# Graph attention, GRU and expert layer: hT's low half first at a tile's end on VectorE, and the normalised x remade on ScalarE

## The chip, the cores and the metric

The kernel runs on one core of a Trainium2 chip. The metric is the device time of one execution in microseconds (us), shown as the median of several executions. The engines are TensorE (PE; PEld are its weight loads), VectorE (DVE), ScalarE (ACT), GpSimd (POOL) and SyncE (SP, which here only issues DMAs). Each runs its own instructions in the order in which they are written, and waits for the others through counted semaphores.

## What is computed

x is 4096 x 256, adj a 4096 x 4096 matrix of zeros and ones. The part that the change touches, with F = 256:

```python
h = layernorm(x)
Wh = h @ W
e = leaky_relu(Wh @ a[:F] + (Wh @ a[F:]).T, 0.2)
att = softmax(where(adj > 0, e, -9e15), axis=1)
h_prime = att @ Wh
gi = h_prime @ w_ih.T + b_ih
gh = h @ w_hh.T + b_hh
r = sigmoid(i_r + h_r); z = sigmoid(i_z + h_z); n = tanh(i_n + r * h_n)
x = x + (1 - z) * n + z * h
# then: layernorm, gate, the top 2 of 16 experts for each token,
# silu(x @ w1) * (x @ w2) @ w3 for each, weighted and added to x
```

## The kernel before

**Tiles and stages.** A first stage normalises x, forms the values and the two terms of the attention logits. The main stage goes over T = 32 tiles of 128 rows, i = 0 to 31, and ends at about 790 us of the span. After it come the routing and the expert products; the change does not touch them.

**Lag.** The main stage is a software pipeline. In iteration i the engines work on the attention of tile i, the logits and the masks of tile i+1, the GRU input of tile i-1 (`combine`, `remake_xn`, `transpose_h`, `copy_hT`, `hT_lo`), the GRU products and the output x1 of tile i-2 (`gru`, `gru_logits`, `gru_n`, `gru_out`), its second layernorm (`norm2`), and the gate of tile i-3 (`transpose_x2`, `copy_x2T`, `gate`, `route_top`, `route_weights`).

**Chunks.** Each tile's attention weights go in CPT = 8 chunks of 512 columns. PE transposes a chunk (L1092), ACT copies its high half to pc (`chunk_hi`, L488), DVE makes its low half (`chunk_lo`, L767, pc<-bank,pc), and PE multiplies it by the values in three terms (L1192 to L1194). Transposes, `chunk_hi` and `chunk_lo` run two chunks ahead of the products: at step c of iteration i, DVE makes chunk c+2, so that steps 6 and 7 make chunks 0 and 1 of the next tile.

**GRU.** PE starts an iteration with `gru(i)`: 12 products of 128x512 (L1218) and 12 of 128x256 (L1223). They read hT, which has a high half (ACT, `copy_hT`) and a low half (DVE, `hT_lo`, L793), made in step 6 of the iteration ahead. hT comes from a transpose of h_prime (hp) and xnb, the normalised x of the tile. xnb is remade from x, which SP loads again from memory (L351), since the first stage's copy was scaled.

**Second layernorm.** `norm2` takes statistics of x1 (L828, L829), writes the variance (var, L830), waits for POOL's power -0.5 (rs, L440), and writes the normalised row xrow (L834). PE transposes it after `gru` (`transpose_x2`).

**Order.** It is written out by hand: the body functions of each engine list what is issued in each step. The last tile and the three iterations behind it are written out separately. Instructions of one engine that depend on each other wait for the writer through `link`.

Of the kernel before, what the change touches and what calls it, by code (L numbers as in the profile page):

```python
# [29 lines left out]
P = 128  # L30
# [5 lines left out]
def gnn_moe(nc, x, adj, W, a, w_ih, w_hh, b_ih, b_hh, gate_w, gate_b, w1, w2, w3, out, rows):  # L36
# [24 lines left out]
    with ctx:  # L61
# [51 lines left out]
        rstd = sb("rstd", [P, T], F32, gs)  # L113
        sS = sb("sS", [P, T], F32, gs)
        bD = sb("bD", [P, T], F32, gs)
        bst = sb("bst", [P, 4, 6], F32, gs)
# [103 lines left out]
        s_plo = sem("weights_lo_done")  # L220
        s_mm = sem("chunk_accumulated")
        s_hp = sem("h_prime_done")
        s_xb = sem("xn_remade")
# [263 lines left out]
        def _(act):  # L487
# [88 lines left out]
            def n_tanh(i):  # L576
                act.wait_ge(s_np, i - 1)
                nc.scalar.activation(nn[:, 0:F], nn[:, 0:F], ACT.Tanh).then_inc(s_nt, 1)

            def copy_hT(i):  # L580
                act.wait_ge(s_th, i)
                if i >= 2:
                    act.wait_ge(s_gru, i - 1)
                act_copy(hT[:, 0, :, :].rearrange("p k m -> p (k m)"), tp[:, :]).then_inc(s_hT, 1)
# [9 lines left out]
            def body(i):  # L594
                if i + 1 < T:
                    for q in range(Q):
                        logits(i + 1, q)
                if live(i, 3):
                    copy_x2T(i)
# [19 lines left out]

            last = (T - 1) * CPT  # L620
            copy_x2T(T - 1)
            chunk_hi(last + 2)
# [11 lines left out]
            gate_exp(T)  # L634
            n_tanh(T)
            copy_hT(T)
            copy_x2T(T + 1)
# [59 lines left out]
        def _(dve):  # L697
# [97 lines left out]

            def remake_xn(n):
                v = n % 2
                dve.wait_ge(s_xr[v], (n // 2) * 16 + 16)
                V_.tensor_scalar(xnb[:, v, :], xin[:, v, :], xmv[:, n, 0:1], rstd[:, n:n + 1], ALU.subtract,
                                 ALU.mult).then_inc(s_xb, 1)  # L800

            def gru_logits(i):
# [21 lines left out]

            def norm2(i):
                u = i % 2
                dve.wait_ge(s_x1, i - 1)
                link(V_.bn_stats(bst[:, 0, :], x1))  # L828
                link(V_.bn_aggr(mv[:, :], bst[:, 0, :]))  # L829
                V_.tensor_scalar(var[:, :], mv[:, 1:2], EPS, None, ALU.add).then_inc(s_var2, 1)  # L830
                dve.wait_ge(s_rs2, i - 1)
                if i >= 4:
# [46 lines left out]
            dve.wait_ge(s_bld, 64)  # L879
            link(V_.tensor_tensor(bias_rz[:, :], bias_rz[:, :], bhh_rz, ALU.add))  # L880
            chunk_lo(0)
            chunk_lo(1)

            def body(i):
# [4 lines left out]
                if live(i, 1):  # L889
                    combine(i - 1)  # L890
                    remake_xn(i - 1)
                if ahead:
# [5 lines left out]
                for c in range(CPT):  # L898
# [13 lines left out]
                    if c == 5 and live(i, 2):  # L912
                        gru_out(i)
                    if c == 6 and live(i, 2):
                        norm2(i)
                    if c == 6 and live(i, 1):
                        hT_lo(i)
                    if i == 0:
                        for n in range(max(2 * c, 5), min(2 * c + 2, 13)):
                            weights_lo(n)  # L920
# [5 lines left out]
            combine(T - 2)  # L926
            remake_xn(T - 2)
            chunk_lo(last + 2)
# [8 lines left out]
            hT_lo(T - 1)  # L937
            chunk_lo(last + 6)
            norm2(T - 1)
            chunk_lo(last + 7)  # L940
            gru_logits(T)
            route_top(T)
            gru_n(T)
            combine(T - 1)
            remake_xn(T - 1)
            route_weights(T)
            hT_lo(T)
            gru_out(T)
            norm2(T)
            gru_logits(T + 1)  # L950
            route_top(T + 1)
            gru_n(T + 1)
            route_weights(T + 1)
            gru_out(T + 1)
            norm2(T + 1)
            route_top(T + 2)
# [434 lines left out]
```

## Time and profile before

| what | value |
|---|---|
| median of 3 runs | 1272.8 us |
| the three runs | 1272.82, 1268.34, 1272.80 us |
| the profiled execution, its own time | 1271.41 us |
| its span | 1269.7 us |
| PE busy in the span | 1158.3 us, 91% |
| DVE busy | 1044.5 us, 82% |
| ACT busy | 777.3 us, 61% |
| POOL busy | 354.0 us, 28% |

The span is what the trace covers, 1.7 us less than the execution's own time. Busy time is the sum of an engine's instructions; shares are of the span. Times in rows are in us from the span's start. A row of the timeline has start, duration, engine, line, operation, output<-input with shapes, a count where several are merged, and in brackets how long the engine sat idle before it and what ended that. Durations of neighbours on one engine can overlap a little, so the distance between two starts tells what an instruction takes of its engine. TensorE's granted clock is 1.00 of its full rate in the main stage's steady part.

### The profile page before, as it was taken

The numbers are of one execution on the slowest core, as the hardware profiler recorded it, in microseconds if no ns is written. First come the engines' busy times: TensorE is split into PE (matmuls) and PEld (weight loads), VectorE is DVE, ScalarE is ACT, GpSimd is POOL, SyncE is SP. The second block draws the span as 40 slices with busy tenths as digits, with TensorE's granted clock in tenths as the row PEclk, the third lists the DMA queues.
The fourth block names the chain that finished last, engine by engine and source line by source line (L and its number), as shares of the span: only waits on it lengthen the run. The fifth ranks groups of instructions, "written<-read, shape, count | busy, mean of one in ns | idle before, by whom it ended". The sixth has DMA issues, their size and how long they took to land.

```text
span 1269.7 us, 25947 instructions
## 1 busy us (share of the span) xinstructions
PE 1158.3 (91%) x7574; PEld 1052.3 (83%) x7575; DVE 1044.5 (82%) x2485; ACT 777.3 (61%) x1125; POOL 354.0 (28%) x351
## 2 busy tenths in 40 slices
PE   5979999999999999999999995379999999999995
PEld 4658989898989999998989894268888888888884
DVE  7957888888989898988888875978888888888883
ACT  3476767667676767676767641036666666666662
POOL 2521111111111111101011100036555555665554
PEclk9779999999999999999999998569999999999998
DMA  8232434343424343433333300232444455435430
GB/s 240 35 58 37 73 60 79 59 80 59 80 59 79 61 72 62 71 64 69 66 69 70 60 22 26 79 105 47 101 96 100 99 140 144 115 78 148 91 50 6
DMA packets 61633, 98.64 MB, mean 78 GB/s; under 512 B 9472, under 2 KB 36096, under 8 KB 61536
## 3 DMA queue, kind: packets, MB, share of 16 engines
q0 software_dynamic: 33600, 52.49, 25.9%
q1 hardware_dynamic: 27936, 44.93, 10.9%
q8 instruction: 52, 0.85, 0.3%
q14 instruction: 45, 0.37, 0.1%
HBM read 213.18 MB, written 18.81 MB: 183 GB/s over the span
## 4 chain that ended last, share of the span: by engine, by line
PE 73%; DVE 18%; issue 3%; ACT 2%; POOL 2%; DMA 1%; DVEq 0%; POOLq 0%
PE bank L1341 17%; PE bank L1092 13%; PE bank L1355 11%; PE bank L1218 8%; PE bank L1193 6%; PE bank L1192 6%; PE bank L1194 6%; PE bank L1223 4%; DVE pc L767 3%; DVE hT L793 2%; ACT pc L488 2%; POOL rs L440 1%; DVE xnv L722 1%; DVE scr L819 1%; DVE scr L820 1%
## 5 line engine op out<-in xcount | busy, mean ns | idle before, releaser
L1192 PE MATMUL bank<-V,pc 128*128 128x258 f32 x1024 | 310.7, 303 | 5.1 <-DVE pc L767 5.1
L1193 PE MATMUL bank<-V,pc 128*128 128x258 f32 x1024 | 290.9, 284 | 0.0
L1194 PE MATMUL bank<-V,pc 128*128 128x258 f32 x1024 | 288.6, 282 | 0.0
L1341 PE MATMUL bank<-wup,xT 128*128 128x512 f32 x948 | 240.3, 402 | 0.9 <-DVE xT L1039 0.9
L488 ACT ACTIVATE pc<-bank 128x512 fp32r<-128x512 f32 x256 | 152.2, 595 | 126.2 <-PE bank L1092 124.7
L767 DVE TENSOR_TENSOR pc<-bank,pc 128x512 fp32r<-128x512 f32 x256 | 175.7, 686 | 57.4 <-ACT pc L488 54.6
L1341 PEld LDWEIGHTS bank<-wup,xT 128*128 128x128 f32 x948 | 174.6, 191 | 35.6 <-DVE xT L1039 1.3
L1192 PEld LDWEIGHTS bank<-V,pc 128*128 128x128 f32 x1024 | 193.5, 189 | 6.2 <-DVE pc L767 6.2
L1193 PEld LDWEIGHTS bank<-V,pc 128*128 128x128 f32 x1024 | 195.5, 191 | 0.0
L1194 PEld LDWEIGHTS bank<-V,pc 128*128 128x128 f32 x1024 | 195.4, 191 | 0.0
L1034 DVE TENSOR_TENSOR wup<-wexp,wup 128x1024 fp32r<-128x1024 f32 x158 | 185.9, 1218 | 2.2 <-ACT wup L488 1.1
L468 POOL DMA_INDIRECT out<-ysc,cidx x79 | 138.8, 1757 | 166.3 <-DMA out<-ysc,cidx 83.0
L488 ACT ACTIVATE wup<-wexp 128x1024 fp32r x158 | 165.8, 1051 | 9.3 <-DMA wexp<-in_L_ffn_w 8.8
L751 DVE CUSTOM_DVE_ANT_0 E<-E,adjb 128x1024 f32<-128x1024 f32 x128 | 155.9, 1218 | 5.3 <-ACT E L537 5.3
L1092 PE MATMUL bank<-ident,E 128*128 128x128 f32 x1024 | 155.3, 275 | 4.9 <-ACT E L542 4.9
L542 ACT ACTIVATE E<-E,nmu 128x1024 f32<-128x1024 f32 x128 | 146.5, 1147 | 19.1 <-DVE nmu L761 19.1
L1355 PE MATMUL bank<-wexp,hidT 128*128 x632 | 149.6, 380 | 0.8 <-ACT hidT L488 0.8
L390 POOL DMA_DIRECT2D adjb<-in_adj x128 | 69.8, 546 | 257.9 <-DVE dmx L751 254.3
L537 ACT ACTIVATE E<-Dp,sS 128x1024 f32<-128x1024 f32 x128 | 136.7, 1141 | 0.2
L1092 PEld LDWEIGHTS bank<-ident,E 128*128 128x128 f32 x1024 | 121.4, 143 | 7.5 <-issue 7.4
L1218 PE MATMUL bank<-wT,hT 128*128 128x512 f32 x384 | 99.4, 409 | 29.4 <-DVE hT L793 29.4
L1355 PEld LDWEIGHTS bank<-wexp,hidT 128*128 128x128 f32 x632 | 114.8, 191 | 13.3 <-issue 1.0
(159 smaller groups left out, 1573.9 us busy)
## 6 DMA issues: line engine op xcount, KB each, us to landing
wexp<-in_L_ffn_w SPq DMA_DIRECT2D x237, 512.0 KB
adjb<-in_adj POOLq DMA_DIRECT2D x128, 256.0 KB, 4.8
token_rows<-xrow SPq DMA_DIRECT2D x32, 130.0 KB, 2.1
E<-in_x SPq DMA_DIRECT2D x8, 512.0 KB, 9.0
xin<-in_x SPq DMA_DIRECT2D x32, 128.0 KB, 2.6
out<-xin SPq DMA_DIRECT2D x32, 128.0 KB, 1.7
xg<-token_rows,gidx POOLq DMA_INDIRECT x79
out<-ysc,cidx POOLq DMA_INDIRECT x79
```

Of the source, the lines that this page charges most:

```text
L488: act_copy = lambda o, i: nc.scalar.activation(o, i, ACT.Copy)
L542: nc.scalar.activation(E[:, n % 2, cols], E[:, n % 2, cols], ACT.Exp, scale=1.0 / LSC, bias=nmu[:, n % 2, 0:1]).then_inc(s_ex, 1)
L751: V_.tensor_tensor_reduce(out=E[:, n % 2, cols], in0=E[:, n % 2, cols], in1=adjb[:, q, :], scale=1.0, scalar=-1e30, op0=ALU.add, op1=ALU.m ...
L767: V_.tensor_tensor(pc[:, C % 3, 1, :], pT[C % 3][:, :], pc[:, C % 3, 0, :].bitcast(F32), ALU.subtract).then_inc(s_plo, 1)
L1034: V_.tensor_tensor(wup[:, r % 2, n, 1, :], wexp[:, one(b), n, :].rearrange("p o f -> p (o f)"), wup[:, r % 2, n, 0, :].bitcast(F32), ALU.s ...
L1092: tr = lambda o, i: nc.tensor.transpose(o, i, ident[:, :])
L1192: mm(acc[:, 0:VW], hi, V[:, j, 0, :], start=j == 0, stop=False)
L1193: mm(acc[:, 0:VW], hi, V[:, j, 1, :], start=False, stop=False)
L1194: ins = mm(acc[:, 0:VW], lo, V[:, j, 0, :], start=False, stop=j == T - 1)
L1218: mm(rzb[:, :], hT[:, a, n, :], wT[:, b, n // KB, n % KB, 0:2 * F], start=n == 0 and (a, b) == (0, 0), stop=n == 2 * KB - 1 and (a, b) == ...
L1341: ins = mm(acc[:, 0:HID], xT[:, r % WR, a, k * P:(k + 1) * P], wup[:, r % 2, n, b, k * HID:(k + 1) * HID], start=(k, a, b) == terms[0], st ...
L1355: ins = mm(accp[:, 0:F], hidT[:, k, :], wexp[:, one(b1), 2, k * F:(k + 1) * F].rearrange("p o f -> p (o f)"), start=k == 0, stop=k == HB - 1)
```

## The change

Three edits.

**DVE's order at the end of a tile.** `norm2` is split into `norm2_statistics` (up to the variance) and `norm2` (from the wait for POOL on). Step 6 was: `chunk_lo`, all of `norm2`, `hT_lo`; step 7 was `chunk_lo`. Step 6 is now: `chunk_lo`, `hT_lo`, `norm2_statistics`; step 7: `chunk_lo`, `norm2`. The code behind the loop is split likewise.

**xnb on ACT.** `remake_xn` goes from DVE (a subtraction and a multiplication by two columns, L799, after `combine`) to ACT (Identity with a scale and a bias for each row), behind the four logits of tile i+1 and ahead of `copy_x2T`. It has one more wait, for x1 of two tiles before, whose step read the same half of xnb.

**The bias.** A new column array nmr, minus mean times deviation's inverse, for all tiles, is made once by one DVE instruction ahead of the first chunk.

```diff
@@ ScalarE @@
+            def remake_xn(n):
+                v = n % 2
+                act.wait_ge(s_xr[v], (n // 2) * 16 + 16)
+                if n == 0:
+                    act.wait_ge(s_nmr, 1)
+                if n >= 2:
+                    act.wait_ge(s_x1, n - 1)
+                nc.scalar.activation(xnb[:, v, :], xin[:, v, :], ACT.Identity, scale=rstd[:, n:n + 1],
+                                     bias=nmr[:, n:n + 1]).then_inc(s_xb, 1)
...
                     for q in range(Q):
                         logits(i + 1, q)
+                if live(i, 1):
+                    remake_xn(i - 1)
                 if live(i, 3):
                     copy_x2T(i)
...
             last = (T - 1) * CPT
+            remake_xn(T - 2)
             copy_x2T(T - 1)
...
             n_tanh(T)
+            remake_xn(T - 1)
             copy_hT(T)
@@ VectorE @@
-            def remake_xn(n):
-                v = n % 2
-                dve.wait_ge(s_xr[v], (n // 2) * 16 + 16)
-                V_.tensor_scalar(xnb[:, v, :], xin[:, v, :], xmv[:, n, 0:1], rstd[:, n:n + 1], ALU.subtract,
-                                 ALU.mult).then_inc(s_xb, 1)
...
-            def norm2(i):
-                u = i % 2
+            def norm2_statistics(i):
                 dve.wait_ge(s_x1, i - 1)
                 link(V_.bn_stats(bst[:, 0, :], x1))
                 link(V_.bn_aggr(mv[:, :], bst[:, 0, :]))
                 V_.tensor_scalar(var[:, :], mv[:, 1:2], EPS, None, ALU.add).then_inc(s_var2, 1)
+
+            def norm2(i):
+                u = i % 2
                 dve.wait_ge(s_rs2, i - 1)
...
+            V_.scalar_tensor_tensor(out=nmr[:, :], in0=xmv[:, :, 0], scalar=-1.0, in1=rstd[:, :], op0=ALU.mult,
+                                    op1=ALU.mult).then_inc(s_nmr, 1)
             chunk_lo(0)
             chunk_lo(1)
...
                     combine(i - 1)
-                    remake_xn(i - 1)
...
-                    if c == 6 and live(i, 2):
-                        norm2(i)
                     if c == 6 and live(i, 1):
                         hT_lo(i)
+                    if c == 6 and live(i, 2):
+                        norm2_statistics(i)
+                    if c == 7 and live(i, 2):
+                        norm2(i)
...
             hT_lo(T - 1)
             chunk_lo(last + 6)
+            norm2_statistics(T - 1)
+            chunk_lo(last + 7)
             norm2(T - 1)
-            chunk_lo(last + 7)
```

In the rows of the built programs below, a name in brackets is a semaphore that the instruction waits for. Line numbers of the changed kernel are higher by 2 to 16. DVE at the end of a tile in the main loop, the kernel before, from the last step of `gru_out` to the first mask of the next iteration:

```order
L823 TENSOR_TENSOR xin<-scr,xin 128x256 [waits x1_stored,dve_link]
L767 TENSOR_TENSOR pc<-bank,pc 128x512 [waits weights_hi_done]
L828 BN_STATS bst<-xin 128x6 [waits x1_done]
L829 BN_AGGR mv<-bst 128x2 [waits dve_link]
L830 TENSOR_SCALAR var<-mv 128x1 [waits dve_link]
L834 TENSOR_SCALAR xrow<-xin,mv,rs 128x256 [waits token_row_stored1,deviation_of_x1_done]
L793 TENSOR_TENSOR hT<-bank,hT 128x512 [waits gru_products_done,hT_copied]
L767 TENSOR_TENSOR pc<-bank,pc 128x512 [waits weights_hi_done]
L745 TENSOR_SCALAR adjb<-adjb 128x1024 [waits adj_loaded0]
```

The same place in the changed kernel:

```order
L833 TENSOR_TENSOR xin<-scr,xin 128x256 [waits x1_stored,dve_link]
L783 TENSOR_TENSOR pc<-bank,pc 128x512 [waits weights_hi_done]
L809 TENSOR_TENSOR hT<-bank,hT 128x512 [waits gru_products_done,hT_copied]
L837 BN_STATS bst<-xin 128x6 [waits x1_done]
L838 BN_AGGR mv<-bst 128x2 [waits dve_link]
L839 TENSOR_SCALAR var<-mv 128x1 [waits dve_link]
L783 TENSOR_TENSOR pc<-bank,pc 128x512 [waits weights_hi_done]
L846 TENSOR_SCALAR xrow<-xin,mv,rs 128x256 [waits token_row_stored1,deviation_of_x1_done]
L761 TENSOR_SCALAR adjb<-adjb 128x1024 [waits adj_loaded0]
```

hT's low half moved ahead of the four instructions of the layernorm, and the second pc stands between the variance and the instruction that waits for POOL.

ACT at the start of an iteration (pc with 128x512 is `chunk_hi`, E<-Dp,sS a quarter of the logits), the kernel before:

```order
L488 ACTIVATE hT<-bank 128x512 [waits gru_products_done,h_transposed]
L488 ACTIVATE pc<-bank 128x512 [waits chunk_accumulated,weights_transposed] x2
L537 ACTIVATE E<-Dp,sS 128x1024 [waits weights_transposed,source_terms_copied]
L537 ACTIVATE E<-Dp,sS 128x1024 x3
L488 ACTIVATE xn2T<-bank 128x256 [waits xn2_transposed]
L488 ACTIVATE pc<-bank 128x512 [waits chunk_accumulated,weights_transposed] x2
```

And in the changed kernel:

```order
L490 ACTIVATE hT<-bank 128x512 [waits gru_products_done,h_transposed]
L490 ACTIVATE pc<-bank 128x512 [waits chunk_accumulated,weights_transposed] x2
L539 ACTIVATE E<-Dp,sS 128x1024 [waits weights_transposed,source_terms_copied]
L539 ACTIVATE E<-Dp,sS 128x1024 x3
L589 ACTIVATE xnb<-xin,nmr,rstd 128x256 [waits x1_done,x_reloaded1]
L490 ACTIVATE xn2T<-bank 128x256 [waits xn2_transposed]
L490 ACTIVATE pc<-bank 128x512 [waits chunk_accumulated,weights_transposed] x2
```

One instruction came in, with its waits for x1 and for the reload of x, between the logits and the copy of the transposed xrow. The built program has two table loads on ACT before and after the change, at the same places.

## Rows read from the trace of the kernel before

**Rows 1.** Busy us of PE, PEld, DVE, ACT, POOL; granted clock; DMA share; GB/s
```profile
300.00:500.00 200.00, 191.24 (x1513) 184.53 (x1513) 176.31 (x460) 137.50 (x197) 25.34 (x47) 1.00 0.39 70
```

**Rows 2.** Waits from 130 to 740 us: waiting instruction, releaser, total, times, longest
```profile
DVE pc L767 <- ACT pc L488: 39.2, 59, 1.4
...
PE bank L1218 <- DVE hT L793: 27.0, 28, 1.1
```

**Rows 3.** Timeline of TensorE: the start of the GRU products in three tiles
```profile
400.96 3.06 PE L1218 MATMUL bank<-wT,hT 128*128 128x512 f32 x12 [0.97 <-DVE hT L793]
...
421.25 0.28 PE L1194 MATMUL bank<-V,pc 128*128 128x258 f32 x1
422.49 3.06 PE L1218 MATMUL bank<-wT,hT 128*128 128x512 f32 x12 [0.96 <-DVE hT L793]
425.39 1.58 PE L1223 MATMUL bank<-wT,hT 128*128 128x256 f32 x12
...
745.36 3.06 PE L1218 MATMUL bank<-wT,hT 128*128 128x512 f32 x12 [0.94 <-DVE hT L793]
```

**Rows 4.** Timeline of TensorE in iteration 2, where gru did not wait
```profile
121.57 0.28 PE L1194 MATMUL bank<-V,pc 128*128 128x258 f32 x1
121.69 2.96 PE L1218 MATMUL bank<-wT,hT 128*128 128x512 f32 x12
124.48 0.76 PE L1223 MATMUL bank<-wT,hT 128*128 128x256 f32 x5
```

**Rows 5.** Timeline of VectorE at a tile's end
```profile
419.32 0.68 DVE L767 TENSOR_TENSOR pc<-bank,pc 128x512 fp32r<-128x512 f32 x1
419.92 0.42 DVE L828 BATCH_NORM_STATS2 bst<-xin 128x6 f32<-128x256 f32 x1
...
420.59 0.15 DVE L830 TENSOR_SCALAR var<-mv 128x1 f32<-128x1 f32 x1
421.42 0.41 DVE L834 TENSOR_SCALAR xrow<-xin,mv,rs 128x256 f32<-128x256 f32 x1 [0.68 <-POOL rs L440]
421.75 0.68 DVE L793 TENSOR_TENSOR hT<-bank,hT 128x512 fp32r<-128x512 f32 x1
```

**Rows 6.** Timeline of VectorE at the next tile's start
```profile
424.21 0.41 DVE L799 TENSOR_SCALAR xnb<-xin,xmv,rstd 128x256 f32<-128x256 f32 x1
424.54 1.22 DVE L751 CUSTOM_DVE_ANT_0 E<-E,adjb 128x1024 f32<-128x1024 f32 x1
```

**Rows 7.** Timeline of ScalarE in one tile, three places
```profile
405.71 0.39 ACT L488 ACTIVATE xn2T<-bank 128x256 f32<-128x256 f32 x1 [2.37 <-PE bank L1092]
...
414.50 0.60 ACT L488 ACTIVATE pc<-bank 128x512 fp32r<-128x512 f32 x1 [0.33 <-PE bank L1092]
...
420.61 4.27 ACT L537 ACTIVATE E<-Dp,sS 128x1024 f32<-128x1024 f32 x4
```

**Rows 8.** Costliest groups of ScalarE: busy and mean ns, idle and releaser
```profile
L488 ACT ACTIVATE wup<-wexp 128x1024 fp32r x158 | 165.8, 1051 | 9.3 <-DMA wexp<-in_L_ffn_w 8.8 <-issue 0.3
...
L542 ACT ACTIVATE E<-E,nmu 128x1024 f32<-128x1024 f32 x128 | 146.5, 1147 | 19.1 <-DVE nmu L761 19.1
...
L578 ACT ACTIVATE scr<-scr 128x256 f32<-128x256 f32 x32 | 13.1, 410 | 3.5 <-DVE scr L812 3.5
```

**Rows 9.** Tile xin from 125 to 765 us: landing of its DMAs, stores and reloads
```profile
DMA to landing us min/median/max: 1.7/2.4/3.3
```

**Rows 10.** Timeline of SyncE's queue: the reload of x in that tile
```profile
420.29 0.45 SPq L351 DMA_DIRECT2D xin<-in_x  x1
```

**Rows 11.** Timeline of the first stage: VectorE and POOL side by side
```profile
28.29 3.78 DVE L722 TENSOR_SCALAR xnv<-E,xmv,rstd 128x256 f32<-128x256 f32 x4
...
28.92 2.02 POOL L406 TENSOR_TENSOR V<-xnv,V 128x1024 fp32r<-128x1024 f32 x1
```

**Rows 12.** Tile rs from 125 to 760 us: POOL's power
```profile
L440 POOL TENSOR_TENSOR rs<-var,mhalf x29: 547/565/576, 140.8 to 743.7; 128x1 f32<-128x1 f32 x29
```

**Rows 13.** Timeline of TensorE in iteration 1
```profile
110.09 0.39 PE L1192 MATMUL bank<-V,pc 128*128 128x258 f32 x1 [2.08 <-DVE pc L767]
```

More of the change, by code:

```diff
@@ L114, in gnn_moe @@
         sS = sb("sS", [P, T], F32, gs)
+        nmr = sb("nmr", [P, T], F32, gs)
         bD = sb("bD", [P, T], F32, gs)
@@ L221, in gnn_moe @@
         s_mm = sem("chunk_accumulated")
+        s_nmr = sem("mean_terms_done")
         s_hp = sem("h_prime_done")
@@ L926, in _ @@
             combine(T - 2)
-            remake_xn(T - 2)
             chunk_lo(last + 2)
@@ L944, in _ @@
             combine(T - 1)
-            remake_xn(T - 1)
             route_weights(T)
@@ L948, in _ @@
             gru_out(T)
+            norm2_statistics(T)
             norm2(T)
@@ L954, in _ @@
             gru_out(T + 1)
+            norm2_statistics(T + 1)
             norm2(T + 1)
```

## The prediction, made before the changed kernel was run

> **What bounds the kernel now.** I read the windows by stage first, then the waits, then one tile of the timeline. From 300 to 500 us PE is busy for 191.24 of 200 us at a granted clock of 1.00, DVE for 176.31 and ACT for 137.50 [rows 1]. PE is thus the bound, with a gap somewhere, and DVE is not far behind. The table of waits says where the gap is: in the main stage PE waits for one thing alone, L1218 for DVE's hT, 28 times, 27.0 us in all [rows 2]. The window ends ahead of one more of the same kind, 0.94 us at 745.36, the last tile's [rows 3]. That makes 29 tiles, each with the same picture.
>
> In that picture hT's low half starts at 421.75 and PE's first GRU product at 422.49, so PE follows hT's start by 0.74 us [rows 3, 5]. Ahead of hT, DVE did the layernorm of x1: statistics at 419.92, variance at 420.59, 0.68 us of idling for POOL, xrow at 421.42 [rows 5]. PE needs none of these for its next 4 us; it stands idle for hT only. hT could have run at 419.92.
>
> The size of the gap is better taken from starts than from idle time, as ends of matmuls are modelled. With the wait, the last attention product starts at 421.25 and L1223 at 425.39, 4.14 us apart [rows 3]. In iteration 2, where nothing was late, the same distance is 124.48 - 121.57 = 2.91 us [rows 4]. The wait therefore costs 1.23 us of a period of 422.49 - 400.96 = 21.53 us [rows 3].
>
> **Part 1: hT before the layernorm.** It removes no work; it puts hT at 419.92 instead of 421.75, 1.83 us earlier. PE could start at 420.66, while its last product starts at 421.25 and the next would follow 0.12 us later (121.69 - 121.57 [rows 4]), at 421.37. hT is then early by 0.71 us, and the wait is gone: 29 x 1.23 = 35.7 us. The bounds of this term are 27.0 + 0.94 = 27.9 us, if only the idle time of the rows goes, and 35.7; I take the upper, since it compares the same two instructions with and without the wait.
>
> What is late next? Every tile is now 1.23 us shorter on PE, so DVE and ACT must keep up. DVE: after hT the statistics start at 420.52, the variance at 421.19 (0.67 behind them, as in rows 5), pc at 421.27. xrow cannot start before 421.19 + 0.83 = 422.02, the distance of variance to xrow in the same rows, now with pc standing in most of POOL's time. From xrow to the first mask it was 424.54 - 421.42 = 3.12 us [rows 5, 6]; out of this go hT and a pc, 0.60 each (a pc and what follows it are 419.92 - 419.32 apart, and hT has the same shape), and the remake of xnb, 0.33 (424.54 - 424.21). So the mask starts at 422.02 + 1.59 = 423.61, 0.93 us earlier than before. PE is 1.23 us earlier, so DVE stands 0.30 us later towards PE.
>
> Two covers take this up. DVE waits for ACT's pc 59 times in 28 tiles, 39.2 us, 1.40 us a tile [rows 2], at steps where ACT waits for PE. And ACT idles 0.33 us for PE before the pc at 414.50 [rows 7], which is the point from which the tile's end is tied to PE again. Beyond 0.33 us, hT's own 0.71 us comes in. In sum DVE may be late by 1.04 us before PE waits; it is late by 0.30. If that cover were gone, each further 0.1 us would cost 2.9 us over 29 tiles.
>
> POOL's power takes 0.565 us [rows 12]. Before, DVE idled beside it; now it runs beside a pc. In the first stage four normalisations took 3.78 us on DVE with a 2.02 us POOL instruction beside them [rows 11], some 2 us more than four of about 0.4 us (the remake is of the same kind, 0.41 [rows 6]), so the two engines can hold each other up. The bounds for the pair here are 0 and 0.57 us a tile; I take 0, as the DVE instruction beside it is another kind, with one operand in PSUM, and even 0.30 + 0.57 = 0.87 stays under 1.04. The Trainium skill (SBUF — State Buffer, Terms) calls the port pair of VectorE and GpSimd an exclusive lock on which the loser fully blocks. By that rule the upper bound holds, by the steady rows nothing is known; the sum is the same by either, but less cover is left, and so the rule bears on the first rival below.
>
> **Part 2: xnb on ACT.** It frees 0.33 us of DVE a tile, already counted. On ACT its price is not in the trace. The nearest rows: a 256-column activation without pointer operands takes 0.410 us, and one column operand adds about 1.147 - 1.051 = 0.096 us at 1024 columns [rows 8]. Two of them give 0.60 us, less some 0.1 us of overlap with its neighbour. Bounds are 0.41 and 1.2 us, twice the estimate. The Trainium skill (ScalarE: Activation LUTs, What ACT_TABLE_LOAD costs) gives 186 ns + 0.833 ns a column + 93 ns for each pointer operand, an estimate of 0.585 us for this one. The same page's rules for kernel authors send multiplications and additions to VectorE rather than ScalarE; per instruction the rows agree (0.41 against 0.60), but here the engine with room decides, and the sum would not differ by that rule.
>
> The instruction goes into ACT's idle stretch. The four logits start at 420.61 and end at 424.88, then ACT idles 2.37 us for PE's transpose of xrow (the tile before: xn2T at 405.71) [rows 7]. With PE earlier by 1.23 and the remake in it, 2.37 - 1.23 - 0.5 = 0.64 us of idling is left. Behind it in ACT's queue stand the copy for the gate and the pc of chunk 2. Its waits: x1 is done before the tile's end. The reload of x is issued at 420.29 [rows 10] and lands after 2.4 us in the median, 3.3 at most [rows 9], by 423.6, while ACT arrives at about 424.8. Cost 0, if the cover holds. Table loads are as many as before in the built program.
>
> In iteration 1 PE waits 2.08 us for a pc that DVE makes behind the remake [rows 13]; 0.33 us less DVE work is worth 0.3 us there, once.
>
> **Part 3: the bias array.** One small DVE instruction, before a chunk for which DVE waits for ACT: nothing. The last tile's separate code keeps its chain: xrow still comes 0.83 us after the variance, with a pc now in POOL's shadow, and the pieces behind it are in the same order. Nothing.
>
> **Sum.** 35.7 + 0.3 = 36.0 us off the profiled execution's own time: 1271.4 - 36.0 = 1235.4 us. The median of the runs is 1.4 us above that execution, so 1236.8 by the median; I give 1236.0.
>
> **Rivals.**
> 1. *A new wait takes a third.* DVE comes later than worked out: 0.30 us by the order, 0.57 by POOL's port, and 0.6 because the remake costs twice my price and holds up the pc of chunk 2 behind it. That is 1.47 against the cover of 1.04, 0.43 us a tile, 12.5 us: 1236.0 + 12.5 = 1248.5. For it: rows 11, and that ACT's cover is thin. Against it: each of the three must be at its worst.
> 2. *It does not do what it says.* hT's order is plain in the built program, but PE's wait might be carried by the chain behind it, ACT's pc to `gru_out` to the last pc, so that an earlier hT meets another late piece: the gain is under 0.5%, about 1270. Against it: chunks 0 and 1 of the next tile are used only after the GRU's 4 us, and no other wait of PE is in the rows.
> 3. *Slower.* The reload of x lands late and ACT, in order, holds the gate's copy and the pc behind it. The point from which it decides: ACT meets it 4.5 us after issue (424.8 - 420.29) and has 0.64 us of idling, and what PE then waits must exceed the 1.23 us gained. So landing must take over 6.4 us in every tile; at 7 us it is 0.6 x 29 = 17 us slower, 1290. Against it: 3.3 us at most in 30 tiles [rows 9].
>
> **How the numbers follow.** The forecast has 0.75, with its own range of 1231 to 1242 (the runs before lie 4.5 us apart, and the idle-time bound of 27.9 us gives 1243). Rival 1 has 0.15, rival 2 0.06, rival 3 0.04. There is no bound on the other side: PE's own work is not touched. The range is 1231 to 1249, the forecast with rival 1 up to its worked price. A measurement of this kernel tells about 0.5% from no change. Faster by more than that: 0.75 + 0.15 = 0.90; within it 0.06; slower 0.04.
>
> **What would show it.** Right: the wait of L1218 for hT is gone in all tiles but the last GRU's, the period is 20.3 us, PE busy is 99% or more in 300 to 500 us; DVE's wait for POOL before xrow falls from 0.68 to under 0.2 us; ACT's idling before xn2T is about 0.6 us; the remake takes 0.6 us. Rival 1 would show as a wait of PE for hT or of DVE for ACT's pc that remains, with a period above 20.5 us. Wrong altogether: a wait of ACT for the reload of x, or a period that stays at 21.5 us.

## The result, and the profile after

| kernel | median of runs | lowest and highest | ratio to before, 95% interval |
|---|---|---|---|
| before | 1272.04 us (6 runs) | 1267.72, 1272.82 | |
| changed | 1232.48 us (6 runs) | 1227.49, 1235.38 | 0.9693 (0.9665 to 0.9722) |

The change makes the kernel 3.1% faster: 39.6 us by the medians, where 36.0 us was forecast. The profiled executions stand at 1271.41 us (span 1269.7) and 1227.49 us (span 1225.7), 44.0 us apart. The profiled execution of the changed kernel is the fastest of its six, so some of its lead is probably not the change's, as argued below.

The main stage first: the windows row of the changed kernel that answers to [rows 1], same columns (busy us of PE, PEld, DVE, ACT, POOL; clock; DMA share; GB/s).

```profile
300.00:500.00 200.00, 200.00 (x1596) 194.54 (x1595) 183.73 (x475) 150.30 (x217) 27.26 (x50) 1.00 0.41 74
```

PE is busy in all of the 200 us, at the same clock, and does 1596 matmuls where it did 1513: 5.5% more in the same time. The waits table of the changed kernel from 130 to 720 us answers to [rows 2] (total, times, longest):

```profile
DVE pc L783 <- ACT pc L490: 35.7, 61, 4.1
ACT xn2T L490 <- PE bank L1108: 20.6, 29, 2.2
ACT E L544 <- DVE nmu L777: 18.2, 28, 0.7
...
ACT xnb L589 <- DMA xin<-in_x: 2.5, 1, 2.5
```

The row of PE waiting for hT, 27.0 us before, is gone. The timeline of PE at the start of the GRU products, which answers to [rows 3], and the last GRU's, where it still waits (the window ended within the row of 403.49, which therefore counts 7 of the 12):

```profile
403.37 0.28 PE L1210 MATMUL bank<-V,pc 128*128 128x258 f32 x1
403.49 1.79 PE L1234 MATMUL bank<-wT,hT 128*128 128x512 f32 x7
...
736.96 3.06 PE L1234 MATMUL bank<-wT,hT 128*128 128x512 f32 x12 [1.41 <-DVE hT L809]
```

The GRU product follows the last attention product after 0.12 us, as in [rows 4]; before, it was 1.24 us [rows 3]. The wait at 736.96 stands behind all tiles; before, the same place had a wait of the same 1.41 us. DVE at the tile's end, in the order of [rows 5] and [rows 6]:

```profile
401.43 0.68 DVE L783 TENSOR_TENSOR pc<-bank,pc 128x512 fp32r<-128x512 f32 x1
402.03 0.68 DVE L809 TENSOR_TENSOR hT<-bank,hT 128x512 fp32r<-128x512 f32 x1
402.63 0.42 DVE L837 BATCH_NORM_STATS2 bst<-xin 128x6 f32<-128x256 f32 x1
...
403.30 0.15 DVE L839 TENSOR_SCALAR var<-mv 128x1 f32<-128x1 f32 x1
403.37 0.68 DVE L783 TENSOR_TENSOR pc<-bank,pc 128x512 fp32r<-128x512 f32 x1
404.14 0.41 DVE L846 TENSOR_SCALAR xrow<-xin,mv,rs 128x256 f32<-128x256 f32 x1
...
405.74 1.22 DVE L767 CUSTOM_DVE_ANT_0 E<-E,adjb 128x1024 f32<-128x1024 f32 x1
```

hT follows its pc at once, and xrow no longer shows an idle time ahead of it: POOL's power ran beside the pc at 403.37. ACT at the next start, which answers to [rows 7]:

```profile
402.73 4.27 ACT L539 ACTIVATE E<-Dp,sS 128x1024 f32<-128x1024 f32 x4
406.88 0.59 ACT L589 ACTIVATE xnb<-xin,nmr,rstd 128x256 f32<-128x256 f32 x1
408.14 0.38 ACT L490 ACTIVATE xn2T<-bank 128x256 f32<-128x256 f32 x1 [0.66 <-PE bank L1108]
...
410.83 0.60 ACT L490 ACTIVATE pc<-bank 128x512 fp32r<-128x512 f32 x1 [1.66 <-PE bank L1108]
```

The remake fits into what was ACT's idle time ahead of xn2T, 2.37 us before and 0.66 us now. And the chain that ended last (the page's part 4), of the kernel before and then of the changed one:

```profile
PE 73%; DVE 18%; issue 3%; ACT 2%; POOL 2%; DMA 1%; DVEq 0%; POOLq 0%
```
```profile
PE 87%; DVE 7%; issue 2%; DMA 2%; ACT 1%; POOL 0%; DVEq 0%; POOLq 0%
```

DVE's and POOL's pieces of the chain have gone over to PE. In the main stage PE is the bound.

**Where the 44.0 us of the profiled spans come from.** The distances are between starts of DVE's hT and of a few marks behind it, taken from the two timelines.

| stretch | before | changed | difference |
|---|---|---|---|
| start to the first hT | 119.79 | 117.83 | -1.96 |
| to the 31st hT, the last tile's | 640.15 | 604.85 | -35.30 |
| to the hT behind all tiles | 13.60 | 13.53 | -0.07 |
| to the routing's index | 61.68 | 60.13 | -1.55 |
| to the last expert slot's xT | 411.50 | 411.06 | -0.44 |
| to the last output-adding DMA of POOL | 17.48 | 12.85 | -4.63 |
| to the end | 5.50 | 5.45 | -0.05 |

The main stage gave 35.3 us. Of the 1.96 us, 1.78 lie ahead of the first pc (at 74.55 us before, at 72.77 after), where nothing was changed. The 4.63 us lie in the drain of the output-adding DMAs at the very end. In the twelve traces of this study that stretch is either 12.9 to 14.1 us or 17.5 to 18.6 us long. It is long in e5, e6, e8 and e11, which have the whole change, and short in e1, e9 and e10; so I take it for scatter and not for a gain. There is one trace a kernel, so that it also varies between executions of one kernel is not shown. The start of the first pc is likewise at 70.9 to 76.9 us over the twelve traces. With the 1.55 us of the fourth stretch (last section) these are 1.78 + 4.63 + 1.55 = 7.96 us, all of the 8.0 by which the profiled spans moved more than forecast. The medians moved by 3.6 us more than forecast: the 1.55 us can account for part of it, the other 2 us are not traced, and the runs of the changed kernel lie 7.9 us apart.

**The period.** The starts of hT in the second and in the last of the steady tiles, of the kernel before and of the changed one:

```profile
141.77 0.68 DVE L793 TENSOR_TENSOR hT<-bank,hT 128x512 fp32r<-128x512 f32 x1
...
744.62 0.69 DVE L793 TENSOR_TENSOR hT<-bank,hT 128x512 fp32r<-128x512 f32 x1
```
```profile
137.96 0.68 DVE L809 TENSOR_TENSOR hT<-bank,hT 128x512 fp32r<-128x512 f32 x1
...
706.73 0.68 DVE L809 TENSOR_TENSOR hT<-bank,hT 128x512 fp32r<-128x512 f32 x1
```

From the second hT to the last of the steady tiles (28 intervals) it is (744.62 - 141.77) / 28 = 21.530 us before and (706.73 - 137.96) / 28 = 20.313 us after: 1.217 us less in each tile. Over 29 tiles that is 35.3 us, what the table has. (hT's own start moves by 1.83 us in the loop and not in the last tile, where it already stood ahead; the end points of the table are free of that.)

### The profile page after: what moved, and what is told of

It reads as the page before. It is cut to its first block, busy times and chain, and to the rows that moved or that the text cites. A ratio compares the mean times of both kernels' runs of the same rounds, so it can differ in the third digit from the quotient of the medians.

```text
span 1225.7 us, 25977 instructions
## 1 busy us (share of the span) xinstructions
PE 1145.8 (93%) x7573; PEld 1050.8 (86%) x7575; DVE 1035.4 (84%) x2454; ACT 792.5 (65%) x1157; POOL 355.3 (29%) x351
## 4 chain that ended last, share of the span: by engine, by line
PE 87%; DVE 7%; issue 2%; DMA 2%; ACT 1%; POOL 0%; DVEq 0%; POOLq 0%
PE bank L1357 18%; PE bank L1108 16%; PE bank L1371 11%; PE bank L1209 10%; PE bank L1208 10%; PE bank L1210 10%; PE bank L1234 7%; PE bank L1239 4%; DMA out<-ysc,cidx 1%; PE bank L1129 1%; PE bank L1260 1%; PE bank L1138 1%; DVE xnv L738 1%; DVE lane_hot L1029 1%; DVE slot_hot L1033 1%
## 5 line engine op out<-in xcount | busy, mean ns | idle before, releaser
L470 POOL DMA_INDIRECT out<-ysc,cidx x79 | 135.1, 1710 | 159.5 <-DMA out<-ysc,cidx 67.5
L544 ACT ACTIVATE E<-E,nmu 128x1024 f32<-128x1024 f32 x128 | 146.5, 1147 | 27.9 <-DVE nmu L777 27.9
L442 POOL TENSOR_TENSOR rs<-var,mhalf 128x1 f32<-128x1 f32 x32 | 18.0, 561 | 375.9 <-DVE var L839 375.9
L461 POOL DMA_INDIRECT xg<-token_rows,gidx x79 | 105.5, 1336 | 71.8 <-DVE cidx L1041 48.0
```

The costliest lines, as they stand in the source:

```text
L544: nc.scalar.activation(E[:, n % 2, cols], E[:, n % 2, cols], ACT.Exp, scale=1.0 / LSC, bias=nmu[:, n % 2, 0:1]).then_inc(s_ex, 1)
```

## The experiments

Theory A is the prediction's reading: each engine has a fixed cover towards PE (0.33 us of ACT's idling and 0.71 us by which hT is early), and DVE work inside it is free. Theory B came from comparing the two traces: what decides is a loop through the engines' queues that is closed from one tile to the next, and the longest of several loops sets the period. Three matter here:

- PE's own work: 20.31 us.
- Loop P, through PE: hT's low half, GRU products, transposes, ACT's pc of chunk 6 (at 414.50, behind its 0.33 us of waiting for PE [rows 7]), the last exponential and the pc of chunk 7 on ACT, DVE's pc of chunk 7, `gru_out`, hT again. Before it is the longest, 21.53 us. With hT 1.83 us earlier it is 19.70 us.
- Loop V, without PE: DVE's row maximum (nmu), ACT's four exponentials with the pcs of chunks 4 to 7 among them in its queue, DVE's pc of chunk 7, `gru_out`, hT, layernorm, pc, masks, row maximum again. Before, ACT's pc at 414.50 could have started at 414.07 had PE's transpose been there (its predecessor, the row below, began at 413.02, and such a pair is 1.05 us apart elsewhere). By these rounded starts V has 0.43 us of room; 0.44 was written down before the runs, and with it V is 21.53 - 0.44 = 21.09 us. Hiding POOL's wait takes 0.60 out of V, moving xnb off DVE 0.33: 20.16 us, only 0.15 under PE's.

```profile
413.02 1.14 ACT L542 ACTIVATE E<-E,nmu 128x1024 f32<-128x1024 f32 x1
```

Diffs are against the changed kernel unless said otherwise. A period is measured in each kernel as above, from the second hT to the last steady one. Ratios are to the kernel before as timed again with each set of runs: median 1271.77 us for e1 to e4, 1270.80 for e5 to e9, 1272.53 for e10 and e11.

### e1: the order alone, xnb stays on DVE

```diff
-                if live(i, 1):
-                    remake_xn(i - 1)
...
                     combine(i - 1)
+                    remake_xn(i - 1)
```

> The new order on DVE alone; xnb stays on DVE, as before, and there is no nmr. The period is the distance of two hT instructions in the steady tiles: 21.53 us before, 20.31 us in the changed kernel. Theory A, the prediction's: DVE may be late by 1.04 us towards PE; here it is late by 0.30 + 0.33 = 0.63 us, so PE does not wait, the period is 20.31 and the move to ACT is worth 0.3 us in all. Theory B, a loop: from row_max (nmu) over ACT's exponentials to the pc of chunk 7, DVE's gru_out, hT, the masks and row_max again there is no PE, and only 0.44 us of waiting in the old order; the loop takes 21.53 - 0.44 = 21.09 us with the old amount of DVE work, 0.60 less without the wait for POOL, 20.49 here. Then the period is 20.49, PE waits 0.1 to 0.2 us a tile for hT, and the move to ACT is worth 0.18 x 29 = 5 us.

Measured: 1237.08 us (1236.09 to 1239.70), ratio 0.9724 (0.9701 to 0.9747), period 20.491 us. The windows row of this kernel, 300 to 500 us, and two of its waits (130 to 720 us):

```profile
300.00:500.00 200.00, 200.00 (x1581) 193.36 (x1580) 184.52 (x479) 142.63 (x207) 26.11 (x48) 1.00 0.39 70
```
```profile
ACT E L544 <- DVE nmu L763: 43.8, 29, 1.6
```

The order alone brings 1.04 of the 1.22 us a tile. The rest, 0.18 us, needs xnb on ACT. B had the value to 0.01 us; A, by which the 0.33 us were covered, falls. PE "busy" is 200.00 in this row too, although it does 15 matmuls fewer than in the changed kernel: small gaps between matmuls vanish in a busy share, and only the count and the period show them. At 400 us of the span ACT's first exponential waits 1.6 us a tile for DVE's row maximum (1.5 in the mean from 130 us on), where the changed kernel has 0.65: that is loop V.

### e2: xnb on ACT alone, the layernorm ahead of hT as before

```diff
+                    if c == 6 and live(i, 2):
+                        norm2(i)
                     if c == 6 and live(i, 1):
                         hT_lo(i)
-                    if c == 7 and live(i, 2):
-                        norm2(i)
```

(`norm2_statistics` also stands ahead of hT.)

> xnb on ACT alone; DVE's order at the tile's end as before, the layernorm with its wait for POOL ahead of hT. Both theories: hT stays 4.7 us behind the pc of chunk 7, which is tied to PE's transposes, so the period stays at 21.53 us and the gain is the 0.3 us of iteration 1, no difference that can be measured (1272). A third view, that relief of DVE carries the gain, expects a period lower by about 0.33 us, 10 us in all.

Measured: 1270.06 us (1266.91 to 1274.04), ratio 0.9994 (0.9972 to 1.0017), period 21.532 us. In its waits from 130 to 720 us PE still waits for hT in every tile:

```profile
PE bank L1234 <- DVE hT L809: 26.0, 27, 1.0
```

By itself the second edit is worth nothing, since loop P is the longest and xnb is not in it.

### e3: hT first, the layernorm whole behind it, xnb on DVE

```diff
                     if c == 6 and live(i, 2):
                         norm2_statistics(i)
-                    if c == 7 and live(i, 2):
+                    if c == 6 and live(i, 2):
                         norm2(i)
```

(With the edit of e1.)

> hT ahead of the layernorm and nothing else: the layernorm stays whole in step 6, DVE idles for POOL, xnb is made on DVE. Theory A: DVE is late by 0.30 + 0.33 + 0.60 = 1.23 us against 1.04, so the period is 20.31 + 0.19 = 20.50 and the gain some 30 us. Theory B: the loop keeps all its work and has only its 0.44 us of waiting to lose, so the period is 21.09, PE waits about 0.8 us a tile for hT, and the gain is 0.44 x 29 = 13 us, about 1259.

Measured: 1255.82 us (1251.73 to 1259.17), ratio 0.9858 (0.9833 to 0.9884), period 21.089 us: B's 21.09, not A's 20.50. Its windows row and three waits:

```profile
300.00:500.00 200.00, 196.69 (x1538) 187.94 (x1538) 179.22 (x468) 139.41 (x204) 24.53 (x45) 1.00 0.38 69
```
```profile
ACT E L544 <- DVE nmu L763: 59.1, 28, 2.2
...
DVE xrow L838 <- POOL rs L442: 19.2, 28, 0.7
...
PEld bank L1227 <- DVE hT L795: 8.8, 26, 0.3
```

To put hT first gives only 0.44 us of the 1.22. The 0.68 us of DVE idling for POOL is again in every tile, and it is in loop V. PE's gaps are now spread over several small waits, of which hT is only one, and none of the rows names the cause; ACT's wait for the row maximum, the largest of the three shown, points at it.

### e4: hT behind the statistics and the variance

```diff
                         gru_out(i)
-                    if c == 6 and live(i, 1):
-                        hT_lo(i)
                     if c == 6 and live(i, 2):
                         norm2_statistics(i)
+                    if c == 6 and live(i, 1):
+                        hT_lo(i)
```

> The changed kernel with hT behind the statistics and the variance instead of ahead of them; xrow still behind the next pc, xnb on ACT. hT then starts 1.35 us later than in the changed kernel, against the 0.71 us by which it was early for PE. Both theories: PE waits for hT again, by 1.35 - 0.71 = 0.64 us of idle, less than before the change; period 21.53 - 0.48 = 21.05 us, gain 14 us, about 1258. If PE's wait for hT were not what bounds the tile, the time would be that of the changed kernel, 1232.

Measured: 1238.17 us (1236.36 to 1244.02), ratio 0.9738 (0.9703 to 0.9773), period 20.454 us, not the expected 21.05. Timelines of DVE and then of PE in this kernel:

```profile
402.32 0.68 DVE L783 TENSOR_TENSOR pc<-bank,pc 128x512 fp32r<-128x512 f32 x1
402.92 0.42 DVE L837 BATCH_NORM_STATS2 bst<-xin 128x6 f32<-128x256 f32 x1
...
403.67 0.69 DVE L809 TENSOR_TENSOR hT<-bank,hT 128x512 fp32r<-128x512 f32 x1
```
```profile
404.26 0.28 PE L1210 MATMUL bank<-V,pc 128*128 128x258 f32 x1
404.42 3.07 PE L1234 MATMUL bank<-wT,hT 128*128 128x512 f32 x12
407.32 1.35 PE L1239 MATMUL bank<-wT,hT 128*128 128x256 f32 x10
```

(The window ended within the last row.)

The miss was a slip in my pricing: 1.35 us is the distance from the pc to hT, but in the changed kernel that is already 0.60, so hT comes 0.75 us later, and loop P gives 19.70 + 0.75 = 20.45 us, which is what was measured. Seen from PE: hT was early by 0.71 us, so 0.04 us of waiting is left, and the GRU's 12 products take 407.32 - 404.42 = 2.90 us instead of 2.79 (124.48 - 121.69 [rows 4]); together 0.15 us. The 0.71 us of the prediction was therefore the right size for hT alone.

### e5 and e6: two more DVE instructions, in the loop and off it

Two instructions of 128x256, each a subtraction and a multiplication by constants, whose result isn't used, in e5 between `combine` and the masks, in e6 behind `route_weights`:

```diff
                     combine(i - 1)
+                    for k in range(2):
+                        V_.tensor_scalar(dump[:, k, :], bias_n[:, 0:F], 1.0, 0.5, ALU.subtract, ALU.mult)
```

> The changed kernel with two more DVE instructions a tile, of the remake's kind and size (0.33 us each), between combine and the masks; their result is not used. Theory A (DVE may be late by 1.04 us, and is by 0.30 + 0.66 = 0.96): the period stays at 20.31 us. Theory B (loop over row_max, ACT's exponentials, gru_out, hT and the masks): the loop of the changed kernel is 20.49 - 0.33 = 20.16 us, 0.15 under PE's 20.31; with 0.66 more it is 20.82, and the period with it, some 15 us in all, 1247.

> The same two DVE instructions a tile behind route_weights, where DVE waits 0.72 us a tile for ACT's pc of chunk 7. Theory B: this place is not on the loop, which passes ACT there, so the period stays at 20.31 us although DVE has as much work as in the run with the two in the loop. If DVE's amount of work mattered and not its place, both would be equally slow.

Measured (one run each, timed once): e5 1241.17 us, period 20.567; e6 1236.37 us, period 20.313. The added work in e5, and ACT's first exponential in that kernel:

```profile
411.05 0.48 DVE L907 TENSOR_SCALAR dump<-bias_n 128x256 f32<-128x256 f32 x2
```
```profile
417.80 1.16 ACT L545 ACTIVATE E<-E,nmu 128x1024 f32<-128x1024 f32 x1 [1.66 <-DVE nmu L778]
```

The next mask starts at 411.45, so the two took 0.40 us of DVE, not the 0.66 I had priced: with constants instead of columns as operands an instruction of this shape takes 0.20 us of the engine, against 0.33 for the old remake [rows 6]. With that, B gives 20.16 + 0.40 = 20.56, measured 20.567; the value I had written, 20.82, was off by the price alone. The same two instructions in e6:

```profile
418.35 0.49 DVE L927 TENSOR_SCALAR dump<-bias_n 128x256 f32<-128x256 f32 x2
...
419.15 0.69 DVE L784 TENSOR_TENSOR pc<-bank,pc 128x512 fp32r<-128x512 f32 x1 [0.32 <-ACT pc L491]
```

In the changed kernel the same pc reads:

```profile
419.42 0.69 DVE L783 TENSOR_TENSOR pc<-bank,pc 128x512 fp32r<-128x512 f32 x1 [0.72 <-ACT pc L490]
```

DVE's idle time ahead of it was 0.72 us and is 0.32 in e6, and the period has not moved. The same work is free at one place and costs 0.25 us a tile at another. DVE's busy time from 300 to 500 us doesn't tell them apart: it is even the higher in e6, 187.43 of 200 us against 184.79 in e5. This pair speaks most plainly for B.

### e8: four more activations behind the remake on ACT

```diff
                     remake_xn(i - 1)
+                    for k in range(4):
+                        nc.scalar.activation(dump[:, k, :], bias_n[:, 0:F], ACT.Identity, scale=rstd[:, 0:1], bias=nmr[:, 0:1])
```

(Their result isn't used.)

> The changed kernel with four more ACT instructions a tile behind the remake, of its kind and size (0.5 us each, 2.0 us); their result is not used. ACT idles 0.66 us there, so the copy for the gate and the pc of chunk 2 come 1.3 us later. PE's gate comes some 1.2 us after the copy, so it waits 0.1 to 0.2 us; the pc of chunk 2 makes DVE 0.7 us later, of which 0.15 are free in the loop. Theory B with that: the period is between 20.4 and 20.9 us. If ACT had room for them, 20.31; if all 2.0 - 0.66 us counted, 21.6.

Measured: 1237.88 us (one run), period 20.38. ACT's timeline shows the added work:

```profile
409.91 2.07 ACT L614 ACTIVATE dump<-bias_n,nmr,rstd 128x256 bf16<-128x256 f32 x4
```

2.07 us more on ACT cost 0.07 us a tile, a little less than the least of what was expected (20.4). ACT had 0.66 us of idling ahead of xn2T and 1.66 ahead of the pc of chunk 3; in e8 these are 0 and 0.71, so they took up most of the work. What is left shows on PE at the gate: its next transposes start 0.44 us behind the start of the gate's products, where in the changed kernel it is 0.36. So a remake at twice its price, which rival 1 feared, would have cost next to nothing.

### e9: the last tile and iteration 1

In the last tile PE's GRU is put ahead of its transpose of xrow; in iteration 1 the low half of chunk 2 is made ahead of the third mask.

```diff
-            transpose_x2(T)
             gru(T)
+            transpose_x2(T)
...
+                    if i == 1:
+                        chunk_lo(i * CPT + 2)
                     mask_logits(i + 1, 2)
```

(The first piece is PE's order in the last tile, the second DVE's in iteration 1, where this `chunk_lo` is left out at its old place.)

> The changed kernel with two small moves at its ends: in the last tile PE transposes xrow behind the GRU products instead of ahead of them, where it waits 0.96 us for xrow; in iteration 1 DVE makes the low half of chunk 2 ahead of the third mask, as PE waits for it there. Worth 1.0 us and up to 1.5 us in the trace, too little for the times to tell from the changed kernel, 1232.

The reason was this row of the changed kernel's PE timeline: xrow now comes after the pc, and in the last tile PE has nothing else between.

```profile
725.84 0.44 PE L1108 MATMUL bank<-ident,xrow 128*128 128x128 f32 x2 [0.96 <-DVE xrow L846]
```

Measured: 1228.49 us (1226.30 to 1230.17), ratio 0.9671 (0.9652 to 0.9689), period 20.313. The last two tiles went from 29.48 to 28.78 us, 0.7 us as meant. Iteration 1 gained 0.07 us: PE's one wait of 1.76 us became two, 0.90 us and, at the next pc, 1.11 us. It has the lowest median of all kernels here, but its interval overlaps the changed kernel's, so only the 0.7 us read from the trace is sure.

### e10 and e11: the same loop, cut on ACT instead

If V is the bound in e3, it must be enough to shorten V anywhere. In e10 (against e3) the last exponential of a tile is moved on ACT from ahead of the pc of chunk 7 to behind it. No work goes away, POOL's wait stays in the open, xnb stays on DVE. e11 is the same edit against e5.

```diff
-                    if 1 <= c < 1 + Q and i + 1 < T:
+                    if 1 <= c < Q and i + 1 < T:
                         weights(i + 1, c - 1)
+                    if c == Q + 1 and i + 1 < T:
+                        weights(i + 1, Q - 1)
```

> The kernel with hT first, the layernorm whole behind it and xnb on DVE (period 21.09 us), and one change on ACT: the last of the four exponentials of the next tile goes behind the pc of chunk 7 instead of ahead of it. Theory B: the exponential's 1.05 us leave the loop over row_max, ACT and gru_out, which falls from 21.09 to 20.04 us; DVE alone needs 21.53 - 0.57 - 0.72 = 20.24 us with its wait for POOL, and PE 20.31. The period is 20.31 us and the time that of the changed kernel or 1 to 2 us under it (1231 to 1237), without the split of the layernorm and without xnb on ACT. Theory A (DVE late by 1.23 us against 1.04, whatever ACT's order): unchanged, 21.09 us, 1256.

> The run with two more DVE instructions in the loop (period 20.57 us), with the same move of the last exponential behind the pc of chunk 7. Theory B: the loop falls by 1.05 us to 19.5 us, the period is PE's 20.31 us. If the two instructions cost time because DVE has no room for them, 20.57 us as before.

Measured: e10 1233.24 us (1230.95 to 1235.17), ratio 0.9702 (0.9678 to 0.9726), period 20.313 against e3's 21.089. e11 1233.49 us (one run), period 20.314 against e5's 20.567. In e10 the waits (130 to 720 us) and ACT's timeline at the moved place read:

```profile
DVE xrow L840 <- POOL rs L442: 19.8, 29, 0.7
DVE pc L771 <- ACT pc L490: 6.4, 5, 3.2
```
```profile
421.05 0.60 ACT L490 ACTIVATE pc<-bank 128x512 fp32r<-128x512 f32 x1
421.54 1.14 ACT L544 ACTIVATE E<-E,nmu 128x1024 f32<-128x1024 f32 x1
```

DVE's 29 waits for POOL are still there, 0.68 us each, and cost nothing now. DVE's wait for ACT, which B puts in the loop, is gone but for five. That confirms the loop: one ACT instruction behind one other gives as much as the whole rest of the change. e10 has no pc between the parts of the layernorm, no activation for xnb and nothing written to the bias array, and can't be told from the changed kernel in time (0.9702 and 0.9693).

### All periods side by side

| kernel | longest loop by B | measured |
|---|---|---|
| before | P 21.53 (given) | 21.530 |
| e2 | P 21.53 | 21.532 |
| e3 | V 21.09 | 21.089 |
| e5 | V 20.16 + 0.40 = 20.56 | 20.567 |
| e1 | V 20.49 | 20.491 |
| e4 | P 19.70 + 0.75 = 20.45 | 20.454 |
| e8 | PE 20.31, and up to 20.9 expected | 20.380 |
| changed, e6, e9, e10, e11 | PE 20.31 | 20.313, 20.313, 20.313, 20.313, 20.314 |

The values for e4 and e5 use the sizes seen in their own traces (written down before the runs were 21.05 and 20.82); those for e1, e2, e3, e6, e10 and e11 were written down before the runs.

## Why the prediction was right

It said 1236.0 us within 1231 to 1249, and the median is 1232.48 us. Point by point:

- **The bound and the gap.** Right. PE's only wait in the steady part was for hT, in 29 tiles, worth 1.23 us each by the distance of starts. Measured is 1.217 us a tile, 35.3 us for the 35.7 of the sum. The lower bound from idle times, 27.9 us, would have been 7 us short: a stalled product also restarts 0.11 us later (e4), and the rest I put down to the modelled ends of matmuls.
- **hT early by 0.71 us.** Right, by e4.
- **DVE 0.30 us later towards PE.** Right: V has 0.44 us of room before and 0.15 us after.
- **The cover of 1.04 us: wrong.** This is the step that failed: "Beyond 0.33 us, hT's own 0.71 us comes in." Lateness on DVE does not stop at hT. It goes on to the next row maximum, to ACT's exponentials and back to DVE one tile on, so it adds up from tile to tile until the loop without PE sets the period; hT being early doesn't help. The room was 0.44 us, and 0.15 was left. In e1, 0.33 us more of DVE costs 0.18; in e5, 0.40 us more costs 0.25. It did not touch the sum, since V stayed under PE's own time, but only by 0.15 us. That the forecast of the time held was therefore in part luck: by the prediction's own account 0.74 us of cover was left over.
- **What each edit is worth.** The prediction gave the whole gain to the order and counted xnb on ACT as room. The runs: hT first 0.44 us a tile (e3), the layernorm split round a pc 0.60 (e1), xnb on ACT 0.18 (e1 against the changed kernel) and nothing by itself (e2).
- **POOL's port, 0 taken out of 0 to 0.57.** Right. POOL's power takes 547, 565 and 576 ns (least, median, most) over 29 tiles beside the pc, the same three values as in [rows 12] without it, and the pc takes 0.68 us as ever. The exclusive lock of the Trainium skill (SBUF — State Buffer, Terms) shows nothing at this pair.
- **The remake on ACT, 0.60 us.** It takes 0.59 us, from 0.587 to 0.602 over 29 tiles; the Trainium skill's formula (ScalarE: Activation LUTs, What ACT_TABLE_LOAD costs) gave 0.585, and this trace agrees. ACT's idling behind it is 0.66 us, forecast 0.64.
- **The reload of x.** Its wait, the mechanism of rival 3, occurs once, in the last tile, where no logits stand ahead of it: 2.51 us, in front of 2.19 us of further idling for PE. It costs nothing.
- **Iteration 1, 0.3 us.** The wait of 2.08 us [rows 13] is 1.76 us in the changed kernel, 0.32 us less. The stretch around it, from the first pc to the first hT, is 0.18 us shorter (45.24 us before, 45.06 after), as 0.13 us was lost ahead of the wait.
- **What was not in the sum.** The GRU behind the last tile, 1.55 us (below); and the two pieces that I take for scatter, 1.8 us ahead of the first pc and 4.6 us at the end, that make the profiled execution look better than the median.

Rival 1's condition was nearer than its chance of 0.15 said. It was ruled out by a sum against 1.04 us; against the true 0.44 us either the port's 0.57 us or 0.15 us more from any other source would have brought it in. Rival 2 was closer in kind: PE's wait was indeed carried by a chain behind it, only 0.44 us of the edit's 1.22 would have been left without the other two parts, and e3 is that case.

## What to carry to other kernels

When an engine's wait was removed here, the next limit was not the slack beside it but the next longest loop through the queues from one tile to the next: follow the releasers backwards from the late instruction until the same instruction of the tile before is met, and add up what has no idle time in it. In this kernel work was free or dear by whether it stood in that loop, not by how busy its engine was (e5 and e6), and to reorder one instruction on another engine of the loop can be worth as much as to remove work (e10). Two edits of which one alone is worth nothing can still both be needed, and a busy share of 100% can hide 1%, which the distance between the same instruction in two tiles shows.

## What the runs showed of the hardware

**TensorE's clock behind the last tile.** The last GRU's products, before and after; the row of before is this one, and that of the changed kernel stands at 736.96 above (3.06 us).

```profile
774.29 4.61 PE L1218 MATMUL bank<-wT,hT 128*128 128x512 f32 x12 [1.41 <-DVE hT L793]
```

The windows over it (columns as in [rows 1]), of the kernel before and of the changed one:

```profile
774.00:776.00 2.00, 1.71 (x5) 1.37 (x6) 1.86 (x6) 0.00 (x0) 0.00 (x0) 0.68 0.00 0
776.00:778.00 2.00, 2.00 (x7) 1.51 (x6) 1.15 (x4) 0.00 (x0) 0.54 (x1) 0.50 0.39 132
```
```profile
738.00:740.00 2.00, 2.00 (x11) 1.64 (x10) 1.34 (x5) 0.00 (x0) 0.45 (x1) 1.00 0.21 70
```

Before, the granted clock is 0.68 and then 0.50 (1.2 GHz), in the changed kernel 1.00 (2.4 GHz). Ahead of it PE had stood idle for 1.15 and 1.41 us before, and for 1.08 and 1.41 us in the changed kernel. This costs or gives 1.55 us. The stretch up to the routing's index is 60.1 us in the changed kernel and in e1, e5, e6, e8, e9, e10 and e11, and 61.7 us before and in e2, e3 and e4. I had not expected it and can't say what decides: the kernels whose PE had waits in every tile are in the slower group, but e4 had hardly any. It is not the 0.07 us between the idle times: e1 has 1.15 us and is in the faster group, e4 has 1.08 us and is in the slower. With one trace of each kernel it is not shown either that it goes by the kernel. That is open.

**Restart after a wait.** 12 GRU products take 2.90 us from first to next group when the first had to wait for its operand, and 2.79 us when it had not ([rows 3 and 4]: 425.39 - 422.49 and 124.48 - 121.69), in e4 with a wait of only some hundredths.

**Column operands on DVE.** 0.20 us against 0.33 us of the engine for 128x256 fp32, with two constants and with two columns (e5 and [rows 6]). The two read different tiles; that the operands make the difference is the likely reading, not tested by itself.

**The drain.** The stretch of output-adding DMAs at the end had two lengths over the twelve traces, 12.9 to 14.1 and 17.5 to 18.6 us, with no tie to the change. The difference is larger than most effects measured here, so stages should be compared, not only spans.
